# Counting without drains, half of the last clique block, and gate weights multiplied ahead, in a four-layer graph network kernel

## The reference

```python
# 6250 nodes, D = 128, 206250 edges sorted by dst, with weights; x (6250, 128)
h = relu(layernorm(x));  x = x + L0(h, W1, b1, W2, b2, edge_weight)   # weighted sum of h[src] by dst
h = relu(layernorm(x));  x = x + L1(h, ...)                           # mean over dst, gelu, graph norm
h = relu(layernorm(x));  x = x + L2(h, x_clique, W, b)                # x_clique[dst] summed by src, mean
h = relu(layernorm(x));  x = x + L3(h, ...)                           # below
...
h = x @ W_in.T + b_in
m = h @ W_msg
agg = segment_sum(m[src], dst)
gi = agg @ W_ih.T + b_ih
gh = h @ W_hh.T + b_hh
r = sigmoid(i_r + h_r); z = sigmoid(i_z + h_z); n = tanh(i_n + r * h_n)
h_new = (1 - z) * n + z * h
return h_new @ W_out.T + b_out
```

## Time and profile before

| what | us |
|---|---|
| median of the runs | 2313.08 |
| profiled execution | 2313.17 |
| its span, first to last instruction | 2311.5 |
| TensorE busy | 2017.3 (87%) |
| TensorE weight loads busy | 1798.2 (78%) |
| VectorE busy | 1538.2 (67%) |
| ScalarE busy | 1229.2 (53%) |
| GpSimd busy | 136.3 (6%) |
| mean granted TensorE clock | 0.941 |

### The profile page before, as it was taken

How to read it: one execution, slowest core, us unless ns; L and a number is a source line. 1 busy time by engine, 2 the same in 40 slices (tenths; PEclk the granted TensorE clock), 3 DMA queues, 4 the chain that set the end, 5 groups by cost and what they waited for, 6 DMA issues and landing times.

```text
span 2311.5 us, 63401 instructions
## 1 busy us (share of the span) xinstructions
PE 2017.3 (87%) x22542; PEld 1798.2 (78%) x22542; DVE 1538.2 (67%) x3147; ACT 1229.2 (53%) x3115; POOL 136.3 (6%) x120
## 2 busy tenths in 40 slices
PE   1169999999999999999989999999985249999897
PEld 1159999999999999999986777778885238888544
DVE  8588888888888888888875666667845840000133
ACT  5756665665656656656636888888864200000242
POOL 5600000000000000000000000000012410000000
PEclk7579999999999999999998999999997569999999
DMA  8412222222222222222233334436831369888121
GB/s 236 119 43 84 98 89 72 97 87 75 97 84 78 97 81 81 97 78 84 97 120 136 121 122 140 150 127 233 312 128 49 110 220 326 300 301 280 50 71 40
DMA packets 184331, 300.85 MB, mean 130 GB/s; under 512 B 12626, under 2 KB 135943, under 8 KB 184159
## 3 DMA queue, kind: packets, MB, share of 16 engines
q1 hardware_dynamic: 180364, 287.55, 36.0%
q0 software_dynamic: 3904, 12.50, 1.9%
HBM read 199.52 MB, written 100.48 MB: 130 GB/s over the span
## 4 chain that ended last, share of the span: by engine, by line
PE 43%; DVE 27%; DVEq 15%; issue 10%; ACT 2%; DMA 2%; POOL 1%; POOLq 0%; ACTq 0%; SPq 0%; PEldq 0%
PE ps L921 23%; DVEq L1725 9%; DVE edge_area L1644 7%; PE ps L905 6%; DVE edge_area L1639 5%; DVE edge_area L1643 4%; PE ps L891 3%; PE ps L821 3%; PE ps L1042 3%; DVE edge_area L1638 2%; PE ps L961 1%; DVE hT_s L1492 1%; DVEq L1638 1%; POOL edge_area L647 1%; PE ps L810 1%
## 5 line engine op out<-in xcount | busy, mean ns | idle before, releaser
L1180 ACT CAST edge_area<-ps 128x392 f16<-128x392 f32 x784 | 398.4, 508 | 423.0 <-PE ps L804 422.6
L821 PE MATMUL ps<-big,rows_area 128*128 128x128 f32 x4802 | 576.9, 277 | 0.3 <-ACT agg_s L1197 0.3
L821 PEld LDWEIGHTS ps<-big,rows_area 128*128 128x128 f32 x4802 | 551.8, 192 | 0.6 <-ACT agg_s L1197 0.6
L810 PE MATMUL ps<-edge_area 128*128 128x98 f16 x6272 | 417.2, 208 | 0.0
L1186 ACT COPY big<-ps 128x392 f32<-128x392 f32 x784 | 407.6, 520 | 0.7 <-PE ps L810 0.5
L1638 DVE TENSOR_TENSOR edge_area<-lo_pair,carry 128x1024 f16<-128x1024 f16 x392 | 271.5, 693 | 130.7 <-issue 103.0
L810 PEld LDWEIGHTS ps<-edge_area 128*128 128x128 f16 x6272 | 332.0, 97 | 0.0
L804 PE MATMUL ps<-edge_area 128*128 128x98 f16 x3136 | 276.2, 209 | 40.1 <-DVE edge_area L1644 36.0
L921 PE MATMUL ps<-big,rows_area 128*128 128x256 f16 (+1 forms) x2450 | 264.6, 272 | 25.9 <-DMA big<-edge_counts 25.9
L921 PE MATMUL ps<-big,agg 128*128 128x256 f16 (+1 forms) x2450 | 279.9, 272 | 0.0
L921 PEld LDWEIGHTS ps<-big,rows_area 128*128 128x128 f16 x2450 | 236.8, 98 | 53.8 <-DMA big<-edge_counts 26.1
(11 more groups left out here) (235 smaller groups left out, 1843.4 us busy)
## 6 DMA issues: line engine op xcount, KB each, us to landing
big<-edge_counts SPq DMA_DIRECT2D x336, 448.0 KB, 4.8
edge_counts<-edge_area SPq DMA_DIRECT2D x49, 1568.0 KB, 5.7
hs<-node_rows POOLq DMA_DIRECT2D x14, 448.0 KB, 4.2
edge_area<-x_stream SPq DMA_DIRECT2D x14, 448.0 KB, 3.9
node_rows<-rows_area SPq DMA_DIRECT2D x1, 3136.0 KB, 13.1
agg_s<-node_rows SPq DMA_DIRECT2D x49, 64.0 KB, 4.9
agg_s<-in_x SPq DMA_DIRECT2D x49, 64.0 KB, 4.4
x_stream<-agg_s SPq DMA_DIRECT2D x49, 64.0 KB, 2.5
```

Of the source, the lines that this page charges most:

```text
L810: last = mm(pair_of(p_weight[s % 4], c), sources_of(slot, r, c), cells_of(oh, slot, r, c), start=(c == 0 and oh is oh_whi), stop=(c == 3 a ...
L821: last = mm(p_sum, h0[:, n, :], w32[:, par, n, :], start=(n == 0), stop=(n == NB - 1))
L1180: nc.scalar.copy(store_slot[:, par, :, cols], p_count[s % 2]).then_inc(sem("count_taken"), 1)
```

## The change

Three parts.

1. In the counting stage the drain between duos is gone. VectorE counts `onehots` up once at the start, and after writing duo j's one-hots it waits for its own weighing of duo j - 2, then does the row operations, then weighs duo j - 1. TensorE's wait moves up by the same one. The row operations are dealt out anew over the duos, `row_T` is at supergroup 7, `lin1` after the last, `row_std` at 3 and a half later; SyncE stores x before it loads the next x row. The end of the loop has one more row in flight, and its operations are woven together.
2. In the last clique block only the lower 128 cliques are flipped, copied and mixed (`parts`); the upper half is still multiplied for the sums and counted, into a count of its own (`out_beyond`).
3. W_in, W_msg and W_ih are multiplied into one matrix per gate before layer 2 (two transposes and five products on TensorE, four copies on ScalarE). In layer 3 the gates take the sums directly; the one-row products are gone, and VectorE adds in-degree times a bias column to each gate (`degree_term`). The in-degrees are loaded spread to all partitions, ahead of the wait for the sums. The loop order is `hidden(i+1)`, `r_gate(i+1)`, `z_gate(i+1)`, `output(i)`, `n_gate(i+1)`.

```diff
-            def half_onehots(h, par, summed=True, last=True, oldest=True, first=False):
+            def half_onehots(h, par, first=False, summed=True, last=True, oldest=True, written=True):
                 for j in range(DUOS):
                     make_onehots(h * DUOS + j, j % RING)
-                    if not (first and j == 0):
-                        weigh_onehots(h * DUOS + j - 1, (j - 1) % RING)
+                    if first and j == 0:
+                        dve.drain()
+                        dve.sem_inc(sem("onehots"), 1)
+                        continue
+
+                    dve.wait_ge(sem("onehots"), h * DUOS + j)
+                    if written and j == 0:
+                        row_rest(h - 5, 1 - par)
                     if oldest:
                         if j == 0:
+                            dve.sem_inc(sem("passed"), 1)
+                            row_mean()
+                        if j == 1:
+                            row_var()
+                        if j == 5:
+                            row_rstd(h - 4)
+                        if j == 6:
                             row_norm(par)
-                        if j == 1:
+                        if j == 7:
                             row_relu(h - 4, par)
-                        if j == 2:
-                            row_rest(h - 4, par)
                     if last:
-                        if j == 0:
+                        if j == 4:
                             add_bias1(h - 3)
-                        if j == 1:
+                        if j == 5:
                             leaky()
-                        if j == 2:
+                        if j == 6:
                             add_x(h - 3, 1 - par)
-                        if j == 3:
+                        if j == 7:
                             row_stats(1 - par)
...
-                    if summed and j == 6:
+                    if summed and j == 7:
                         prod1(h - 2, par)
-                    dve.drain()
+                    weigh_onehots(h * DUOS + j - 1, (j - 1) % RING)
...
-                    pe.wait_ge(sem("onehots"), h * DUOS + s // 2 + 1)
+                    pe.wait_ge(sem("onehots"), h * DUOS + s // 2 + 2)
...
-                        if rows and s == 3:
+                        if rows and s == 7:
                             row_T(h - 2, par)
...
-                        if rows and s == 11:
+                        if rows and s == SGS - 1:
                             lin1(h - 2, par)
...
-                    if s == 9 and normed:
-                        row_std(h - 3)
+                    if s == 3 and normed:
+                        row_std(h - 4)
...
                 def half(h, b, par, older=True):
                     load_h_row(h - 1, 1 - par)
+                    store_x(h - 3, 1 - par)
                     load_x_row(h - 2, par)
-                    store_x(h - 3, 1 - par)
```

```diff
-                def flip(n, k, par):
-                    for c in range(2):
+                def flip(n, k, par, parts):
+                    for c in range(parts):
...
-                        last.then_inc(sem("flips"), 1)
+                        last.then_inc(sem("flips"), 2 // parts)
...
-                        for c in range(2):
+                        for c in range(parts):
                             for l in range(2):
                                 last = mm(p_mix[:, lo:hi], xc_plane[:, par, c, l, :], flipped[:, odd, c, lo:hi],
-                                          start=(c == 0 and l == 0), stop=(c == 1 and l == 1))
+                                          start=(c == 0 and l == 0), stop=(c == parts - 1 and l == 1))
...
-                            last = nc.scalar.activation(unused[:, j, 0:width, :], piece[:, par, k, 0:width, j, :], ACT.Copy,
-                                                        accum_out=out_part[:, par, sh:sh + 1])
+                            if parts == 2:
+                                last = nc.scalar.activation(unused[:, j, 0:width, :], piece[:, par, k, 0:width, j, :],
+                                                            ACT.Copy, accum_out=out_part[:, par, sh:sh + 1])
+                                continue
+                            for c, counts in enumerate((out_part[:, par, :], out_beyond[:])):
+                                last = nc.scalar.activation(unused[:, j, c, :], piece[:, par, k, c, j, :], ACT.Copy,
+                                                            accum_out=counts[:, sh:sh + 1])
```

```diff
+            nc.tensor.transpose(pD[:, 0:D], wt["Wmsg"][:], ident[:])
+            nc.tensor.transpose(pD[:, D:2 * D], wt["WinT"][:], ident[:]).then_inc(sem("fold_made"), 1)
+            pe.wait_ge(sem("fold_taken"), 1)
+            mm(pD[:, TILE:TILE + 3 * D], flipped_w[:, 0:D], wt["WihT"][:], start=True, stop=True).then_inc(sem("fold_made"), 1)
+            pe.wait_ge(sem("fold_taken"), 2)
+            for g in range(3):
+                mm(pD[:, 3 * D + g:3 * D + g + 1], msg_gates[:, g * D:(g + 1) * D], b_in[:], start=True, stop=True)
+            mm(pD[:, 0:3 * D], flipped_w[:, D:2 * D], msg_gates, start=True, stop=True).then_inc(sem("fold_made"), 1)
             pe.sem_inc(sem("lin3"), 1)
...
-                wide(pC, [(wt["WinT"][:], step_view(agg, i)),
-                          (bias["b_in_row"][:], step_view(deg_row, i, slice(0, 1)))]).then_inc(sem("hid_sum"), 1)
...
-                wide(pD, [(wt["Wmsg"][:], fixed_view(ah_s))]).then_inc(sem("msg_sum"), 1)
...
             with pe.Fori(0, NS - 1) as i:
-                gates(i)
                 hidden(i + 1)
+                r_gate(i + 1)
+                z_gate(i + 1)
                 output(i)
-                messages(i + 1)
-            gates(NS - 1)
+                n_gate(i + 1)
...
             sp.dma_start(hs[:], rows_of(rows_dram, 0)).then_inc(sem("h_in4"), 16)
+            sp.dma_start(deg_all, deg_dram[:, 0:NPAD].to_broadcast([P, NPAD])).then_inc(sem("deg_row_in"), 16)
             sp.dma_start(xs2[:, 0:W].rearrange("p (b d) -> p b d", d=D), rows_of(x_dram, 0)).then_inc(sem("x_in4"), 16)
             sp.wait_ge(sem("agg_done"), 3)
-            sp.dma_start(deg_row[0:1, :], deg_dram[:, 0:NPAD]).then_inc(sem("deg_row_in"), 16)
...
+            def degree_term(out, i, g, sums):
+                return V.scalar_tensor_tensor(out=out, in0=deg_all[:, bass.ds(i * W, W)], scalar=b_deg[:, g:g + 1],
+                                              in1=sums[:, 0:W], op0=ALU.mult, op1=ALU.add)
```

More of the change, by code:

```diff
@@ L1049, in fixed_view, with hidden @@
                 return lambda lo, n: v[:, lo:lo + n]
-            def hidden(i):
+            U, hh = wt["WihT"], wt["WhhT"]
+            def hidden(i, first=False):
                 pe.wait_ge(sem("h_in4"), i * 16 + 16)
-                pe.wait_ge(sem("r_ready"), i + 1)
-                transposes(pA, flat(hs)).then_inc(sem("hT"), 1)
+                if not first:
+                    pe.wait_ge(sem("z_sum"), i)
+                transposes(pB, flat(hs)).then_inc(sem("hT"), 1)
                 pe.wait_ge(sem("hT_s"), i + NS + 1)
-                pe.wait_ge(sem("z_ready"), i + 1)
-                wide(pB, [(wt["WinT"][:], fixed_view(hT_s))]).then_inc(sem("hidden"), 1)
-                pe.wait_ge(sem("n_in"), i + 1)
-                wide(pC, [(wt["WinT"][:], step_view(agg, i)),
-                          (bias["b_in_row"][:], step_view(deg_row, i, slice(0, 1)))]).then_inc(sem("hid_sum"), 1)
@@ L1066, in messages, with r_gate @@
-            def messages(i):
-                pe.wait_ge(sem("hid_sum_s"), i + 1)
-                wide(pD, [(wt["Wmsg"][:], fixed_view(ah_s))]).then_inc(sem("msg_sum"), 1)
-            def gates(i):
-                ih, hh = wt["WihT"], wt["WhhT"]
+                if not first:
+                    pe.wait_ge(sem("n_taken"), i)
+                wide(pC, [(wt["WinT"][:], fixed_view(hT_s))]).then_inc(sem("hidden"), 1)
+            def r_gate(i, first=False):
+                halves = ((0, TILE), (TILE, W))
+                if not first:
+                    pe.wait_ge(sem("r_sum"), i)
+                for lo, hi in halves:
+                    mm(pA[:, lo:hi], U[:, 0:D], step_view(agg, i)(lo, hi - lo), start=True, stop=False)
@@ L1738, in row_sum, with row_end @@
                 row_var()
-            def row_planes(g, par):
+            def row_end(g, par):
+                row_rstd(g)
+                dve.drain()
                 row_norm(par)
@@ L1786, in count_sorted @@
                 V.memset(pick_row[:, DEG_BLOCKS - 1:DEG_BLOCKS], 1.0).then_inc(sem("bad_known"), 1)
-                row_planes(NB - 4, 1)
-                row_sum(NB - 3, 0)
-                prod1(NB - 2, 1)
-                row_end(NB - 3, 0)
-                row_sum(NB - 2, 1)
-                prod1(NB - 1, 0)
-                row_end(NB - 2, 1)
-                row_sum(NB - 1, 0)
+                add_x(NB - 3, 0)
+                row_rstd(NB - 4)
+                dve.drain()
+                row_stats(0)
```

(42 more changed lines are left out.)

186 lines of the change are left out of this document (109 added, 77 removed).

## The result

The changed kernel takes 2260.20 us (median; 2255.18 to 2261.03, 4 runs), against 2313.18 for the kernel before beside it: ratio 0.9767, interval 0.9751 to 0.9784. That is 53 us less, where 77.5 were forecast; 2260.2 lies above the range of 2225 to 2257. The profiled execution is 2261.03 us, its span 2259.4, the granted clock 0.935.

What follows compares the result with a forecast made beforehand. TensorE was taken as nearly full, with VectorE's drains holding the counting stage above TensorE's pace. Terms of -29, +1.5, -6.5, +1.5 and -45 sum to -77.5, taking 2313.2 to 2235.7 us; range 2225 to 2257.

Steps and rivals of the forecast that it cites:

- The drains: Counting stage: without drains between duos VectorE falls below TensorE's 21.08 us per half, so TensorE sets the pace; -29 us.
- The added self-wait and the new order of the rows' chain: Counting stage: VectorE's wait for its own older weighing and the re-dealt row operations are covered; cost 0.
- End of the counting stage: After the counting loop: one more row's steps are woven into the exposed final chain; +1.5 us (0 to +5).
- Last clique block: Layer 1: half the flips and mixes go, pieces shrink from 3.82 to 2.85 us, ScalarE becoming slower; -6.5 us.
- The fold: Before layer 2's first clique step: multiplying the gate weights together is partly exposed; +1.5 us (0 to +4).
- The last stage: Layer 3's gates: steps fall from 19.86 to 14.3 us on TensorE and the stage begins earlier; -45 us (-38 to -47).
- the degree row: Beginning of the last stage: the 3.2 MB in-degree load is done before its first use; 0, up to +5 us.
- the chain through VectorE and ScalarE: Last stage's step: this dependency loop ends 4.9 us after the transpose began, hidden by 0.1 us behind TensorE's 5.0.
- The third: Rival, last stage: the chain through VectorE and ScalarE bounds steps at 17 us, +16, so 2252 us; chance 13%.

Runs made afterwards that it cites:

- e4_drain_back: The changed kernel with an explicit drain put back after each weighing on VectorE, new order and self-wait kept: 2289.13 us, ratio 0.9895.
- e5_no_sums: The changed kernel with layer 0's neighbour sum cut to the first and last of each twelve or thirteen products, sums incomplete: 2110.29 us, one run.
- e1_load_first: The changed kernel with SyncE sending for the next h rows ahead of the previous step's output store in the last stage: 2228.73 us, ratio 0.963.
- e6_filled_wait: The changed kernel, SyncE's order kept, with TensorE doing 8 unread products ahead of its wait for h rows in the last stage: 2251.33 us, ratio 0.9728.
- e7_deg_late: e1_load_first with the weight fold moved behind layer 2's last step and the degree row sent for only after the sums: 2229.38 us, ratio 0.9634.
- e3_both_halves: The changed kernel with the last clique block's upper half flipped, copied, mixed and counted as before: 2268.48 us, ratio 0.9799.

## Why the prediction was wrong

*The drains*: right, -29.1. TensorE's 21.07 is the ceiling, as rows 3 said. The price of one drain was mis-sized (0.17 to 0.30 taken, 0.40 to 0.44 measured), which did not matter because the ceiling cut it. The size matters only for the next change that frees TensorE. The Trainium skill, VectorE: DVE Perf Modes, section "The DRAIN you can't avoid", was read in the prediction as saying that this saves nothing; e4_drain_back and e5_no_sums show that it does not hold for these operations. The same section sends the reader on for operations that nothing holds, which start earlier, and with that half of it the traces agree.

*The added self-wait and the new order of the rows' chain*: costed at nothing, right. TensorE's count products wait 11.7 us for VectorE over the whole stage, and in e5_no_sums VectorE has no gap.

*End of the counting stage*: forecast +1.5, measured -0.3. The woven chain of VectorE's operations behind the last row's product takes 5.2 us instead of 4.9, so the steps woven in cost it a few tenths; TensorE's part ahead of it is 0.5 us shorter.

*Last clique block*: -6.5 forecast, -7.6 measured. ScalarE's own pace was sized well (2.98 measured, 2.85 forecast), but it begins the block ahead: its waits of 0.79 and 0.68 us in the first two pieces are a lead that it gives up by some 0.3 a piece, so TensorE keeps its own 2.67 for three pieces before ScalarE holds it up. I took the slower engine's pace for all seven. By TensorE's own work alone the block would gain 7 x 1.15 = 8.0 us; ScalarE takes back 0.4 of it, where I had 1.3.

*The fold*: +1.5 forecast, +1.2 measured in the changed kernel, up to +1.7 in the runs that have the fold in the same place.

*Layer 1's dense part* took 1.7 us more. TensorE waits 4.97 us for h rows there (4.73 before), and the granted clock rises 5.8 us after that wait instead of 3.2. It varies from run to run: from the end of layer 1's last product to the last clique's product are 67.4 us before, 69.1 in the changed kernel, and 67.2 to 68.3 in e1_load_first to e4_drain_back, e6_filled_wait and e7_deg_late, which have the change's code in this place. Three of them are within 0.2 us of the kernel before, so I take the 1.7 for chance and not for a cost of the change.

*The last stage*: this is the step that failed. I wrote "The step becomes 19.86 - 5.52 = 14.3 us on TensorE" and counted VectorE's nine operations and the loop through ScalarE, but not SyncE's queue. The change moves the output of a step from before the messages to near the end of it. Before, 2195.65 - 2183.17 = 12.5 us lay between the output's start and the next transposes, enough for addition, store and load one after another; with the output so late 4.7 to 4.9 us lie there (e1_load_first, whose load does not depend on it), and that chain takes some 8.4 (8.2 to 8.7). The order on SyncE, store(i) before load(i + 2), was harmless before and is not named in the diff. I looked for what stands behind a moved wait on VectorE, and for counting's queue on SyncE, but not here. With the queue turned every other part of this term held: 12.7 for the first interval, 14.4 for the rest, the degree row hidden, the chain through VectorE and ScalarE hidden, -45.8 in all.

Of the rivals none had this place. The third named steps of 17 us and gave 2252, by the chain through VectorE and ScalarE, which e1_load_first clears. Beside TensorE's time a second loop existed, but through DMA. Had the loop through SyncE been costed with what e6_filled_wait shows, 3.6 us for the wait and 2.0 for the clock in five intervals are +28 us, and the forecast would have been 2264, 4 us above the measurement. (The last step's own slow clock, 31.97 us from its transposes to the end against 29.65 in e1_load_first, would add 2.3 more.)

## What to carry to other kernels

When a step is moved, list for each queue what stands behind the wait that it releases, the DMA queues above all: a store that waits for late work holds every load issued after it. Where one loop prefetches and stores, issue the load first. The wait named at the first TensorE instruction of a step tells it at once.

## What the runs showed that I had not expected

A wait for 3.6 us costs more than itself: the seven transposes and the hidden rows after it run at a granted clock of 0.50, which costs 2.0 us a step on average. In e3_both_halves, after waits of 3.61 and 3.31 us, the first two sets of transposes still took 0.98 us, and the slow work came behind them (after the first, hidden rows 3.35 us and reset product 3.17, where 1.77 and 1.67 are usual), for steps of the same length, 20.8 and 21.0. So the clock fell after such waits in every run of this order that did not fill them, but not always at the same instruction. The waits of 1.0 us for ScalarE in each step do not lower it: in e1_load_first the granted clock is 1.00 from 2130 to 2190 (busy time of that stretch):

```profile
2130.00:2190.00 60.00, 55.99 (x203) 31.01 (x202) 44.28 (x38) 27.15 (x26) 7.18 (x3) 1.00 0.31 89
```

VectorE and GpSimd get in each other's way. In e1_load_first GpSimd's addition (L735) and VectorE's (L2102) fall together in some steps (timelines of the two engines):

```profile
2133.63 1.09 DVE L2102 TENSOR_TENSOR edge_area<-big 128x896 f32<-128x896 f32 x1
2148.20 2.89 DVE L2102 TENSOR_TENSOR edge_area<-big 128x896 f32<-128x896 f32 x1
...
2177.16 1.09 DVE L2102 TENSOR_TENSOR edge_area<-big 128x896 f32<-128x896 f32 x1
```

```profile
2148.07 2.07 POOL L735 TENSOR_TENSOR edge_area<-edge_area,bc_bout 128x896 f32 x1 [25.04 <-DMA edge_area<-x_stream]
...
2177.16 3.03 POOL L735 TENSOR_TENSOR edge_area<-edge_area,bc_bout 128x896 f32 x1 [12.58 <-DMA edge_area<-x_stream]
```

VectorE's addition of 1.09 us takes 2.89 when GpSimd's began just before it, and ends 0.95 us after that one; where both start together GpSimd's takes 3.03 instead of 2.07. This fits one waiting for the other to end, and not the two sharing. It costs nothing here, since VectorE is busy for 44.28 of 60 us in this stage, and TensorE sets the step. The Trainium skill, Trainium Architecture — The Big Picture, section "What this means for kernel authors", calls the ports that the two engines share an exclusive lock, and the trace agrees.
